# A ViT tower with routed layers: where a tile's up weights are rounded, and the order of gathers and roots behind layer 2

## What is computed

```python
def moe_ffn(x2d, gw, w1, w2):
    vals, idx = jax.lax.top_k(x2d @ gw, 2)
    gsc = jax.nn.softmax(vals, axis=-1)
    ...
    for each expert e:  acc += cw[:, e, None] * (gelu(x2d @ w1[e], approximate=False) @ w2[e])
...
y = jax.nn.relu(nx @ ffn_wi[i]) @ ffn_wo[i]          # dense part, in all four
if i in (1, 3):
    y = y + moe_ffn(nx.reshape(-1, d), gate_w[mi], moe_w1[mi], moe_w2[mi]).reshape(b, s, d)
h = h + y
```

## Time and profile before

| | us |
|---|---|
| median of 3 runs | 1929.55 |
| lowest, highest | 1923.34, 1930.13 |
| the profiled execution | 1929.32 |
| its span, first to last instruction | 1927.5 |
| PE, DVE, ACT, POOL busy | 1611.0, 1066.9, 776.8, 549.6 |

### The profile page before, as it was taken

How to read it: one execution, slowest core, us unless ns; L and a number is a source line. 1 busy time by engine, 2 the same in 40 slices (tenths; PEclk the granted TensorE clock), 3 DMA queues, 4 the chain that set the end, 5 groups by cost and what they waited for, 6 DMA issues and landing times.

```text
span 1927.5 us, 33597 instructions
## 1 busy us (share of the span) xinstructions
PE 1611.0 (84%) x11901; PEld 1489.6 (77%) x11901; DVE 1066.9 (55%) x2975; ACT 776.8 (40%) x1843; POOL 549.6 (29%) x1292
## 2 busy tenths in 40 slices
PE   5888798793989998999978999588989998899970
PEld 5777676792777997988878889588888987788960
DVE  4564457232655676567764343377755668434436
ACT  1433432341343553454433444244534544254420
POOL 2244335004754112612340000453234123300030
PEclk8765766896577998999888999879989989899995
DMA  4120101451069000100014666200010000256630
GB/s 143 33 73 10 43 17 38 126 164 56 26 202 275 30 2 17 62 2 6 16 34 147 213 196 198 71 15 1 1 62 18 1 16 15 63 184 209 204 91 28
DMA packets 78393, 149.75 MB, mean 78 GB/s; under 512 B 6340, under 2 KB 57843, under 8 KB 78230
## 3 DMA queue, kind: packets, MB, share of 16 engines
q1 hardware_dynamic: 71894, 135.35, 21.9%
q0 software_dynamic: 6336, 12.26, 2.2%
HBM read 106.59 MB, written 41.05 MB: 77 GB/s over the span
## 4 chain that ended last, share of the span: by engine, by line
PE 51%; issue 18%; DVE 15%; DMA 6%; ACT 5%; POOL 3%; SPq 1%; another core or an unknown queue 0%; DVEq 0%; POOLq 0%; ACTq 0%
PE ps_proj L1034 10%; PE ps_proj L1157 5%; PE ps_score L1228 5%; PE ps_proj L1048 5%; PE ps_o L1129 4%; PE ps_pt L999 4%; DMA w_in<-w_all_dram 4%; PE ps_proj L1211 4%; PE ps_score L1085 3%; PE ps_score L1096 3%; PE ps_o L1119 3%; ACT w_hi L1362 2%; PE ps_proj L1015 1%; DVE prob L1536 1%; DVE w_lo L1697 1%
## 5 line engine op out<-in xcount | busy, mean ns | idle before, releaser
L1228 PE MATMUL ps_score<-w,hid 128*112 128x192 f32 (+2 forms) x1680 | 305.1, 334 | 8.9 <-DVE x L1847 8.9
L1228 PEld LDWEIGHTS ps_score<-w,hid 128*112 128x112 f32 (+2 forms) x1680 | 277.0, 180 | 11.3 <-DVE x L1847 10.8
L1352 ACT ACTIVATE hid<-ps_proj 128x224 f32<-128x224 f32 (+2 forms) x360 | 133.6, 382 | 265.7 <-PE ps_proj L1211 258.9
L1440 POOL TENSOR_SCALAR tmp<-rs,var 111x1 f32<-111x1 f32 x110 | 40.9, 372 | 583.8 <-DVE rs L1510 583.0
L1401 POOL DMA_INDIRECT tin<-rows_out,idx x66 | 68.1, 1032 | 484.9 <-issue 379.9
L999 PE MATMUL ps_pt<-const,prob 111*111 111x111 f32 x660 | 129.3, 315 | 34.2 <-ACT probt L1340 22.4
L1157 PE MATMUL ps_proj<-wo,ot 128*111 128x192 f32 (+1 forms) x616 | 138.9, 375 | 4.0 <-ACT ot L1318 3.7
L999 PEld LDWEIGHTS ps_pt<-const,prob 111*111 111x111 f32 x660 | 96.2, 205 | 55.0 <-issue 27.2
L1340 ACT ACTIVATE probt<-ps_pt 111x333 f32<-111x333 f32 x176 | 78.9, 448 | 131.1 <-PE ps_pt L999 130.5
L1129 PEld LDWEIGHTS ps_o<-v,probt 111*111 111x111 f32 x1056 | 128.9, 195 | 0.5
L1332 ACT ACTIVATE prob<-prob 111x333 f32<-111x333 f32 (+1 forms) x209 | 102.6, 493 | 58.6 <-DVE prob L1539 40.0
(11 more groups left out here) (250 smaller groups left out, 4172.1 us busy)
## 6 DMA issues: line engine op xcount, KB each, us to landing
w_in<-w_all_dram SPq DMA_DIRECT2D x65, 768.0 KB, 4.3
w<-w_all_dram SPq DMA_DIRECT2D x50, 576.0 KB, 5.0
rows_in<-zero SPq DMA_DIRECT2D x1, 12320.0 KB, 47.8
rows_out<-zero SPq DMA_DIRECT2D x1, 9240.0 KB, 80.5
tin<-rows_in SPq DMA_DIRECT2D x36, 224.0 KB
rows_out<-tout SPq DMA_DIRECT2D x36, 168.0 KB
patch<-patches_dram SPq DMA_DIRECT2D x11, 333.0 KB, 3.0
wo<-wo_all_dram SPq DMA_DIRECT2D x6, 576.0 KB, 3.8
```

The lines of the kernel that those rows point to most:

```text
L1228: last = pe.matmul(bank[0:n, 0:C], hid[:, i % 2, m, at:at + n], w2[:, slot, m, :], start=(m == 0), stop=(m == FC - 1))
L1352: act.activation(hid[:, i % 2, m, 0:n], bank[:, 0:n], ACT.Relu if b.tile is None else ACT.Gelu).then_inc(taken, 1)
```

## The change

Only `routed_order` changes, so only the order of steps.

```diff
@@ routed_order, the loop over tiles k, n = 18
-            if m == 2 and (k < n or not last):
-                out.append(("W1", r + k + 2))
+            if m == 2 and k == 0:
+                out.append(("W1", r + 2))
+            if m == 5 and k + 3 <= n + (1 if last else 3):
+                out.append(("W1", r + k + 3))
             if k and m in (2, 5):
                 out.append(("D", 1 + k, m // 3))
-    out += [("GAT", 0), ("GAT", 1), ("GAT", 2), ("GAT", 3)]
+    out += [("GAT", 0), ("GAT", 1), ("GAT", 2)] + ([("GAT", 3)] if last else [])
     for m in range(FC):
         out.append(("U", 3 + n, m))
         if m % 2:
             out.append(("D", 2 + n, m // 2))
-        if m >= (1 if last else 2) and (last or m < 5):
-            g = m - (1 if last else 2)
-            out += [("COMB", g), ("GAT", g + 4)]
-        if m == 2 and not last:
-            out.append(("W1", r + n + 3))
-    out += [] if last else [("W1", r + n + 4), ("next", ("A", 0))]
+        if last and m:
+            out += [("COMB", m - 1), ("GAT", m + 3)]
+        if not last and m > 3:
+            out.append(("COMB", m - 4))
     out.append(("D", 3 + n, 0))
-    out += [] if last else [("next", ("A", 1))]
+    out += [] if last else [("COMB", 2)]
     out.append(("D", 3 + n, 1))
-    out += [] if last else [("next", ("A", 2))]
+    out += [] if last else [("next", ("A", 0)), ("next", ("A", 1)), ("W1", r + n + 4), ("GAT", 3), ("next", ("A", 2)),
+                            ("GAT", 4), ("GAT", 5), ("GAT", 6)]
```

## The result

| | median us | runs | lowest to highest |
|---|---|---|---|
| kernel before | 1922.05 | 20 | 1907.19 to 1931.85 |
| changed kernel | 1935.74 | 20 | 1928.23 to 1952.85 |

The changed kernel takes 1.008 times the time of before (95% interval 1.0059 to 1.0101), some 15 us more. The forecast was 1932 us and +2.9 us. 1935.74 lies inside its range, but the outcome that the forecast gave most chance to, no measurable change, is wrong: the kernel is slower by more than 0.5%. Two errors met. The sum was made against a profiled execution of before of 1929.3 us, 7 us over the median that 20 runs give; and the change costs some 10 us more than the sum.

What follows compares the result with a forecast made beforehand. The prediction took the 8.58 us turn around the single `w_in` buffer to bound the tiles. Layer 4's +4.6 us and layer 2's -1.7 us (7.5 - 9.2) gave +2.9 us on 1929.3: 1932 us, range 1924 to 1941.

Steps and rivals of the forecast that it cites:

- store to first gather: End of layer 2: a `w_in` load issued just ahead of the last store delays the first gather by 0.5 us.
- gathers and roots: End of layer 2: six gathers and three roots take 18.8 instead of 27.96 us, 9.2 us saved.
- tiles of layer 4: Layer 4's tile loop: half tile 3.9, clock 0.5 and slip at the end 0.2, together +4.6 us.
- What bounds the tiles: Tile loops: the load and rounding turn around the single `w_in` buffer, 8.58 us, sets the pace, not TensorE's 8.03.
- first rival: Tile loops: rounding is covered, TensorE's idle time goes, turn falls to 8.03 us, total 1899 us; chance 0.05.
- The half tile lost once a layer: End of tile 0: the added rounding waits for its load; +3.9 us in layer 4, part of layer 2's delay.
- clock term: Behind the new idle stretch of some 5 us TensorE works at 1.2 GHz; +0.5 us a layer, bounds 0 and 2.0.
- Do the later ones delay `w_in`? I take 0: SP's queue: store and `w` closer behind `w_in` cost its load 0; bounds -0.1 to +0.2 us a load.
- third rival: The loads collide: store and `w` closer behind `w_in` cost 0.25 us a load, total 1941 us; chance 0.12.
- DVE ... costs nothing in the loop: Tile loop: second `tout` copy stands behind both `w_lo`, but TensorE needs its bank half a tile later; cost 0.
- SP ... keep their order: Tile loop: `w_in`, the store of `tout`, the loads of `w` and `tin` keep their order in SP's queue.
- The gathers: End of layer 2: last store waits behind the second attention load's rounding, so gathers start at 1211.0, 7.5 us later.

Runs made afterwards that it cites:

- g0: The kernel before, run again unchanged as a control and profiled a second time; ratio 0.9995.
- e2: Kernel before with only the three roots in a row at the end of layer 2, every rounding in its old place; ratio 0.9997.
- e1: Kernel before with only the new rounding places at tile ends; gathers, combines and roots in their old order; ratio 1.0118.
- g1: Changed kernel with the second attention load's rounding back at the middle of layer 2's last block; ratio 1.0062.
- f3: Kernel before with each rounding kept mid-tile but one load further ahead, so TensorE stands a whole tile back; ratio 1.013.
- g2: Changed kernel with three buffers for `w` instead of two and one more load of `w` ahead; ratio 1.0104.
- f1: Changed kernel with the tile-end rounding behind the down product, so store and `w` load go out before the waiting `w_in` load; ratio 1.0333.
- e4: Changed kernel with two `w_in` buffers, each load issued one rounding further ahead; ratio 0.9976.
- f2: f1's order (rounding behind the down product at a tile's end) with two `w_in` buffers; ratio 0.994.
- e5: Kernel before with two `w_in` buffers and three roots in a row, every rounding in its old place; ratio 0.9941.
- e3: Kernel before with two `w_in` buffers, each load issued one rounding further ahead, everything else in its old place; ratio 0.9947.

## Why the prediction was right and wrong

The measured stages against the sum. Old order: mean of the profiles of before, g0 and e2, for the gathers and the attention stage of all with the old tail. New order: changed, e1 and for layer 4 also g1; for gathers and attention all with roots in a row.

| term | predicted | measured |
|---|---|---|
| tiles of layer 2 to the last store | +7.0 | 183.8 - 174.0 = +9.8 |
| store to first gather | +0.5 | 4.7 - 3.1 = +1.6 |
| gathers and roots | -9.2 | 20.9 - 29.6 = -8.7 |
| attention stage | 0 | 446.9 - 444.0 = +2.9 |
| tiles of layer 4 | +4.6 | 180.1 - 172.3 = +7.8 |
| sum | +2.9 | +13.4 |

The measured sum agrees with the ratio (+11 to +19 us). Its weakest term is the attention stage: the two groups of profiles overlap (444.4 to 450.6 against 440.4 to 447.2).

**What bounds the tiles** was right. Two buffers take the wait away and the turn falls to TensorE's pace. The fit from which the first rival's 3.8 us were estimated is stated by the Trainium skill (DMA: Bandwidth & Descriptors, Anatomy of one DMA) for transfers that GpSimd issues; `w_in` is issued by SyncE, and no stage's mean here is below 4.24 us.

**The half tile lost once a layer** was right: TensorE idle 5.2 us between tiles 0 and 1 of layer 2 and 4.1 us in layer 4, and with twice the lag tiles 4 pay a whole tile (f3). Its clock term was a little small: the gap between the `w_hi` at the stall and the next is 8.9 to 10.0 us in the changed kernel and e1, against a mean turn of 8.8, so some 0.1 to 1.2 us a layer for the 0.5 taken. How much of it is due to the longer idle stretch stays open, since with the old order the stretch at 1.2 GHz was 0, 3.4 and 6.8 us long (g0, before, e2).

**"Do the later ones delay `w_in`? I take 0"** is the step that failed most. The mean load is 4.54 us over eight layer stages with the new places (changed, e1, g1, g2: 4.43 to 4.64) and 4.31 us over eight with the old (before, g0, e2, f3: 4.24 to 4.49). That is 0.22 us a load, just at the upper bound given; the turn grows by 0.27 us, over 17 turns 4.5 us a layer. Two things are in it: the median load of a stage rises by 0.15 us (4.28 to 4.43, means of the eight), and loads of over 5 us are 13 of 139 with the new places, 1 of 140 with the old. I had set the term to 0 by comparing two single loads, one of 4.00 and one of 4.91 us, whose scatter of 0.9 us is four times the effect. The third rival had the mechanism and the size (0.25 us a load, 1941 us) and got a chance of 0.12. That the distance to store and `w` is the cause is argued, not shown: the distance did shrink by 0.37 us in each turn, and f1 shows that these transfers can cost `w_in` 2.2 us from ahead, but no run changed the distance alone. f3 rules out the longer lead: with it and the old distances the loads stay at 4.24 and 4.27 us. By ring order alone a transfer issued behind `w_in` would not delay it; no run here settles how they share the engines.

**"DVE ... costs nothing in the loop", "SP ... keep their order"** was true in the changed kernel and too narrow. The order is kept, but `w` now goes out some 5 us after its slot is free (5.3 in e4), and once the loads are out of the way it costs some 0.3 us in each tile (e4 against f2).

**The gathers.** Held as predicted (store at 1207.38, 1207.4 worked out); the load ahead of the store costs 1.6 us and not 0.5. **The roots** save 8.7 us where 9.2 were taken. That the saving is kept stood nowhere as a step, and was assumed: 2.9 us go back in the attention stage, 1.9 of them in its first twelve evictions, and most of those in a gap on ACT that the clock doesn't explain. What the three roots in a row are worth in the end stays open: nothing by e2 (0.9997), 1 us by e5 against e3, 7 us by the changed kernel against e1 (1.008 and 1.0118, overlapping intervals), and 5.8 by the table. From layer 2's first `tin` to the end the profiles with them are shorter in each pair: e2 by 3.5 us or more, the changed kernel by 6.8 (909.5 against 916.3), e5 by 4.0 (878.2 against 882.2).

**The base.** Before's profile was 7 us over its median of 20 runs, with loads of 4.49 us in layer 2. I took 1929.55 us, the median of three, for the kernel's time, and gave the range 8 us below and 9 above. The time hit the range by luck, because one error offset the other: +2.9 on 1929.3 gives 1932, and +13.4 on 1922 gives 1935. Against 1922.05 the same sum would have given 1925 and the same range 1917 to 1934, and 1935.74 lies above it.

## What to carry to other kernels

Where one buffer's load sets the pace, every transfer on the same queue is a part of its time: take the mean of all loads of the stage, not of two, and work out what a few tenths of a us would cost over all turns before setting them to zero. A transfer is paid by the one issued right behind it if that has the critical reader, so write down the queue's order beside who waits for each entry. A stage's gain counts only at the end of the next: here some 2 of 8.7 us were gone ten us later. And where two profiles of one kernel differ by 9 us, a forecast of 3 us can't be read off one of each.

## What the hardware showed

After 5.2 us without a matmul TensorE worked some 6 us at 1.2 GHz in the changed kernel. A long idle stretch isn't needed for it: e2 has some 6.8 us at 1.2 GHz at the same place behind gaps of 1.4 and 1.0 us, and g0, behind the same gaps, none. Behind the stage of gathers and roots, in whose last 20 us TensorE was busy for 7.5 to 9.6 us (five profiles), the first 2.5 us of projections ran at 1.2 GHz in all thirteen profiles. In each kernel with 12 or more runs the time falls as the mean granted clock rises, 0.5 to 1.5 us for each 0.001.

A load of 768 KB takes 4.0 to 4.9 us in most turns, but 5.5 to 6.3 us now and then (6.15, 6.09 and 5.49 in the changed kernel's profile, 6.30 once in g0's). With 576 KB issued 1.13 us ahead of it, it takes 6.4 to 7.0 us (f1).

No version of this study with one `w_in` buffer beats the kernel before. With two buffers e3, e5 and f2 do, by 0.5 to 0.6%.
